# A decoder layer: a zero column ahead of the attention's keys, packed bytes moved as 32-bit words, and the 384-column tile's values issued earlier on TensorE

## The reference, cut to what matters

```python
q = (x @ Wq).reshape(B, T, H, Dh)
k = (x @ Wk).reshape(B, T, H, Dh)
v = (x @ Wv).reshape(B, T, H, Dh)
scores = jnp.einsum('bthd,bshd->bhts', q, k)
mask = jnp.tril(jnp.ones((T, T), dtype=scores.dtype))
scores = scores * mask
attn = jax.nn.softmax(scores / T ** 0.5, axis=-1)
out = jnp.einsum('bhts,bshd->bthd', attn, v).reshape(B, T, H * Dh)
...
low = W_packed & 15
high = W_packed >> 4 & 15
```

## Time and profile before

| | |
|---|---|
| median of three runs | 1464.04 us |
| the profiled execution: its own time | 1464.93 us |
| the profiled execution: its span | 1463.2 us |
| TensorE busy | 1418.3 us, 97% |
| VectorE, ScalarE, GpSimd busy | 992.6, 711.9, 386.7 us |
| exponentials (L1269) | 256, and 256 reads of their sums |
| `exp_zero` (L1278) | 48 |
| pack casts on ScalarE and VectorE | 16 each |
| conversions of bytes on GpSimd (L759) | 96 |

### The profile page before, as it was taken

How to read it: one execution, slowest core, us unless ns; L and a number is a source line. 1 busy time by engine, 2 the same in 40 slices (tenths; PEclk the granted TensorE clock), 3 DMA queues, 4 the chain that set the end, 5 groups by cost and what they waited for, 6 DMA issues and landing times.

```text
span 1463.2 us, 26832 instructions
## 1 busy us (share of the span) xinstructions
PE 1418.3 (97%) x8896; PEld 718.8 (49%) x8896; DVE 992.6 (68%) x2125; ACT 711.9 (49%) x1648; POOL 386.7 (26%) x703
## 2 busy tenths in 40 slices
PE   6999999999999999999999999999999999999999
PEld 4466457456645644344444444444444444444444
DVE  7796788679568868885675566666666665766533
ACT  5795289249527944345344353353353343443432
POOL 0054225305473545421121121211112112212100
PEclk9999999999999999999999999999999999999999
DMA  7554612452556601010100100001001001000011
GB/s 252 136 173 122 177 67 89 126 145 67 157 147 182 206 32 45 17 33 17 33 17 17 33 17 17 23 12 35 17 17 33 17 17 33 17 17 1 1 58 58
DMA packets 77310, 98.01 MB, mean 67 GB/s; under 512 B 8049, under 2 KB 60785, under 8 KB 76785
## 3 DMA queue, kind: packets, MB, share of 16 engines
q1 hardware_dynamic: 77168, 96.23, 21.5%
HBM read 68.94 MB, written 27.26 MB: 66 GB/s over the span
## 4 chain that ended last, share of the span: by engine, by line
PE 87%; DVE 5%; ACT 4%; issue 3%; DMA 0%; POOL 0%; DVEq 0%; ACTq 0%; POOLq 0%; SPq 0%
PE bank L888 25%; PE bank L890 25%; PE bank L889 25%; PE bank L952 3%; PE bank L973 2%; ACT prob L1269 2%; PE bank L941 2%; PE bank L982 1%; PE bank L901 1%; PE bank L1013 1%; PE bank L1028 1%; PE bank L1023 1%; DVE xt L1595 1%; ACT pk_t L1303 1%; DVE bank L1610 1%
## 5 line engine op out<-in xcount | busy, mean ns | idle before, releaser
L888 PE MATMUL bank<-xs,G 128*128 128x512 f16 x896 | 339.8, 379 | 2.1 <-DVE c L1741 0.9
L889 PE MATMUL bank<-xs,G 128*128 128x512 f16 x896 | 339.6, 379 | 0.0
L890 PE MATMUL bank<-xs,G 128*128 128x512 f16 x896 | 339.6, 379 | 0.0
L1741 DVE TENSOR_TENSOR c<-bank,c 128x512 f32<-128x512 f32 x128 | 88.1, 689 | 193.0 <-PE bank L890 193.0
L1355 ACT COPY c<-bank 128x512 f32<-128x512 f32 x192 | 111.4, 580 | 220.4 <-PE bank L890 215.5
L888 PE MATMUL bank<-Wd,hid 128*128 128x512 f16 x512 | 194.1, 379 | 2.8 <-DVE X L1795 2.8
L889 PE MATMUL bank<-Wd,hid 128*128 128x512 f16 x512 | 194.0, 379 | 0.0
L890 PE MATMUL bank<-Wd,hid 128*128 128x512 f16 x512 | 194.0, 379 | 0.0
L751 POOL TENSOR_TENSOR c<-c,m 128x512 f32<-128x512 f32 x64 | 82.4, 1288 | 388.5 <-ACT c L1355 388.5
L1795 DVE SCALAR_TENSOR_TENSOR X<-bank,col,X 128x512 f32<-128x512 f32 x128 | 95.3, 749 | 101.6 <-PE bank L890 101.5
L1610 DVE CUSTOM_DVE_ANT_0 bank<-bank,mask,col 128x128 f32<-128x128 f32 (+3 forms) x256 | 139.2, 548 | 21.3 <-PE bank L941 12.1
(11 more groups left out here) (196 smaller groups left out, 2397.4 us busy)
## 6 DMA issues: line engine op xcount, KB each, us to landing
stack<-qk_dram SPq DMA_DIRECT2D x128, 128.0 KB, 3.3
sc_in<-scale_t SPq DMA_DIRECT2D x30, 384.0 KB
qk_dram<-qk SPq DMA_DIRECT2D x32, 256.0 KB, 3.1
packed_t<-pk_t SPq DMA_DIRECT2D x32, 192.0 KB, 2.0
pk_in<-packed_t SPq DMA_DIRECT2D x30, 192.0 KB
X<-in_x_dram SPq DMA_DIRECT2D x4, 1024.0 KB, 6.1
pk_in<-L_ffn_gate_W_packed_dram SPq DMA_DIRECT2D x16, 256.0 KB, 2.8
pk_in<-n_L_ffn_up_W_packed_dram SPq DMA_DIRECT2D x16, 256.0 KB, 3.1
```

The costliest lines, as they stand in the source:

```text
L888: pe.matmul(o, lhs(0), rhs(0), start=first, stop=False, skip_group_check=onto)
L889: pe.matmul(o, lhs(0), rhs(1), start=False, stop=False, skip_group_check=onto)
L890: return pe.matmul(o, lhs(1), rhs(0), start=False, stop=stop, skip_group_check=onto)
L1741: nc.vector.tensor_tensor(dst[:], bank[at][:], dst[:], ALU.add).then_inc(comb, 1)
```

## The change

1. The keys get two zero columns ahead of each head's 512. For the three narrower tiles the score matmul begins one column early, so column 0 of the bank is the score 0 and the keys follow in columns 1 to `wide`. `row_max` works on columns 1 and up, the exponential on all `wide + 1`, so that `prob[..., 0]` is exp(-max) and the sum holds it once. `exp_zero`, `e_zero` and its semaphore go. `all_tokens` and `masked_values` read `prob[..., 0]`, the turns read their blocks one column further on, and each exponential from the third unit on waits for `den_done` and `v_zero_done` of two units before. GpSimd clears the zero columns once.
2. `convert` adds 1024 to each byte in place of the plain cast, so the fp16 value holds the byte in its low eight bits. `repacked` on ScalarE copies 384 fp32 words instead of casting 768 columns, `repacked` on VectorE copies 768 fp16 columns without a cast.
3. `recips` and `values` of the 384-column tile (units 2, 6 and 10, `sooner`) are issued after the turn of the third head of the 512-column tile, ahead of its fourth head and of the next unit's fourth scores. The slots are counted accordingly.

```diff
-        stack = sb("stack", [P, 2, HEADS, T], F16)
+        stack = sb("stack", [P, 2 * HEADS * T + 2 * HEADS], F16)
+        queries = stack[:, 0:HEADS * T].rearrange("p (h t) -> p h t", h=HEADS)
+        keys = stack[:, HEADS * T:].rearrange("p (h t) -> p h t", h=HEADS)
...
         def turn_slot(h):
-            return h + 2 * (max(0, h - 2) // 16) + max(0, h // 4 - 1)
+            return h + 2 * (max(0, h - 2) // 16) + max(0, h // 4 - 1) + int(h % 16 == 15 and h < ROWS - 1)
...
+        def sooner(u):
+            return u % TT == TT - 2 and u < UNITS - 2
+
         def recip_slot(u):
-            return turn_slot(4 * u + 7) + 1 if u < UNITS - 1 else pack_slot(HG - 1, 1) + 1
+            if u == UNITS - 1:
+                return pack_slot(HG - 1, 1) + 1
+            return turn_slot(4 * u + (6 if sooner(u) else 7)) + 1
...
-                        sp.dma_start(stack[32 * part:32 * part + 32, which, 4 * c:4 * c + 4, :],
+                        sp.dma_start((queries, keys)[which][32 * part:32 * part + 32, 4 * c:4 * c + 4, 2 * which:2 * which + T],
...
+            pool.wait_ge(w_lo, W_PARTS)
+            nc.gpsimd.memset(keys[:, :, 0:2], 0.0).then_inc(zero_keys, 1)
...
-                nc.gpsimd.tensor_copy(pk_16[:, a], pk_in[:, a].bitcast(U8).rearrange("p (c four) -> p c four", four=4)[:, :, 0]).then_inc(pk_conv, 1)
+                nc.gpsimd.tensor_scalar(pk_16[:, a], pk_in[:, a].bitcast(U8).rearrange("p (c four) -> p c four", four=4)[:, :, 0],
+                                        BYTES, None, ALU.add).then_inc(pk_conv, 1)
...
-                    pool.wait_ge(e_zero_done, beyond_units(n, u - 2))
...
-                pool.wait_ge(e_zero_done, beyond_units(n, u))
+                pool.wait_ge(exp_done, n * ROWS + 4 * u + 4)
...
-                                        e_zero[:, u % 2, :].unsqueeze(2).to_broadcast([P, 4, DH]), ALU.mult).then_inc(v_zero_done, 1)
+                                        prob[:, u % 2, :, 0:1].to_broadcast([P, 4, DH]), ALU.mult).then_inc(v_zero_done, 1)
...
-                pe.matmul(bank[j][:, 0:wide[i]], stack[:, 0, h, P * i:P * i + P], stack[:, 1, h, 0:wide[i]],
+                pe.matmul(bank[j][:, 0:wide[i] + beyond[i]], queries[:, h, P * i:P * i + P], keys[:, h, 2 - beyond[i]:2 + wide[i]],
...
-                    mm = pe.transpose(turn_bank(slot)[:, P * k:P * k + P], prob[:, u % 2, j, P * k:P * k + P], ident[:])
+                    at = P * k + beyond[i]
+                    mm = pe.transpose(turn_bank(slot)[:, P * k:P * k + P], prob[:, u % 2, j, at:at + P], ident[:])
...
-                        if j == 3 and u > 0:
+                        if j == 2 and u > 0 and sooner(u - 1):
+                            recips(n, u - 1)
+                            values(n, u - 1)
+                        if j == 3 and u > 0 and not sooner(u - 1):
                             recips(n, u - 1)
                             if u < UNITS - 1:
                                 values(n, u - 1)
...
                 if u >= 2:
                     act.wait_ge(t_full, n * ROWS + 4 * (u - 2) + j + 1)
-                nc.scalar.activation(prob[:, u % 2, j, 0:wide[i]], bank[j][:, 0:wide[i]], ACT.Exp,
-                                     bias=nmx[:, u % 2, j:j + 1], accum_out=den[:, u % 2, j:j + 1]).then_inc(exp_done, 1)
-
-            def exp_zero(n, u):
-
-                if u >= 2:
                     act.wait_ge(den_done, beyond_units(n, u - 2))
                     act.wait_ge(v_zero_done, beyond_units(n, u - 2))
-                act.wait_ge(shift_done, n * ROWS + 4 * u + 4)
-                nc.scalar.activation(e_zero[:, u % 2, :], nmx[:, u % 2, :], ACT.Exp).then_inc(e_zero_done, 1)
+                nc.scalar.activation(prob[:, u % 2, j, 0:wide[i] + beyond[i]], bank[j][:, 0:wide[i] + beyond[i]], ACT.Exp,
+                                     bias=nmx[:, u % 2, j:j + 1], accum_out=den[:, u % 2, j:j + 1]).then_inc(exp_done, 1)
...
-                nc.scalar.copy(pk_t[:, 0], turn_bank(pack_slot(r, 0))[:].bitcast(F16)[:, 0:HALF]).then_inc(pk_out0, 1)
+                nc.scalar.copy(pk_t[:, 0].bitcast(F32), turn_bank(pack_slot(r, 0))[:, 0:HALF // 2]).then_inc(pk_out0, 1)
...
-                        if j == 3 and u % TT < TT - 1:
-                            exp_zero(n, u)
...
-                nc.vector.tensor_copy(pk_t[:, 1], turn_bank(pack_slot(r, 1))[:].bitcast(F16)[:, 0:HALF]).then_inc(pk_out1, 1)
+                nc.vector.tensor_copy(pk_t[:, 1].bitcast(F16), turn_bank(pack_slot(r, 1))[:].bitcast(F16)[:, 0:HALF]).then_inc(pk_out1, 1)
```

More of the change, by code:

```diff
@@ L137, in decoder_layer @@
         v_beyond = sb("v_beyond", [P, TT - 1, D], F32)
-        w_raw = stack[:].rearrange("p a h t -> p (a h t)").bitcast(F32).rearrange("p (w k n) -> p w k n", w=4, k=KT)
+        w_raw = stack[:, 0:2 * HEADS * T].bitcast(F32).rearrange("p (w k n) -> p w k n", w=4, k=KT)
         xn = sb("xn", [P, TT, D], F32)
@@ L152, in decoder_layer @@
         r_den = sb("r_den", [P, 2, P], F32)
-        e_zero = sb("e_zero", [P, 2, 4], F32)
         v_zero = sb("v_zero", [P, 2, P], F32)
@@ L223, in decoder_layer @@
         c11 = [sb2(f"c11_{x}", [P, T], F32) for x in range(2)]
+        sb2("beside_zero_keys", [P, HEADS], F32)
         G[1] = sb2("G1", [P, 7, 2, 4, P], F16)
@@ L250, in decoder_layer @@
         qkv_full, qk_hi, qk_lo, v_out = (sem(n) for n in ("qkv_full", "qk_hi", "qk_lo", "v_out"))
-        vb_full, vb_out, e_zero_done, v_zero_done = (sem(n) for n in ("vb_full", "vb_out", "e_zero_done", "v_zero_done"))
+        vb_full, vb_out, zero_keys, v_zero_done = (sem(n) for n in ("vb_full", "vb_out", "zero_keys", "v_zero_done"))
         stacked = [sem(f"stacked{i}") for i in range(4)]
@@ L277, in decoder_layer @@
         wide = [(i + 1) * P for i in range(TT)]
+        beyond = [int(i < TT - 1) for i in range(TT)]
         def turn_slot(h):
-            return h + 2 * (max(0, h - 2) // 16) + max(0, h // 4 - 1)
+            return h + 2 * (max(0, h - 2) // 16) + max(0, h // 4 - 1) + int(h % 16 == 15 and h < ROWS - 1)
         def copied_by_act(u):
@@ L317, in decoder_layer @@
         AHEAD = 4
+        BYTES = 1024.0
         CONTEXT_BANK = (6, 4, 5, 7)
@@ L930, in scores @@
                 hg, i = u // TT, u % TT
+                if n + u + j == 0:
+                    pe.wait_ge(zero_keys, 1)
                 if i == 0 and j == 0:
@@ L1608, in row_max @@
                 alone(dve, s_full, n * ROWS + 4 * u + j + 1)
-                nc.vector.tensor_tensor_reduce(out=bank[j][:, 0:wide[i]], in0=bank[j][:, 0:wide[i]],
+                own = slice(beyond[i], beyond[i] + wide[i])
+                nc.vector.tensor_tensor_reduce(out=bank[j][:, own], in0=bank[j][:, own],
                                                in1=mask[:, P * (3 - i):P * (3 - i) + wide[i]], scale=C_EXP,
@@ L1626, in all_tokens @@
                     dve.wait_ge(exp_done, n * ROWS + 4 * u + 4)
-                    dve.wait_ge(e_zero_done, beyond_units(n, u))
-                    nc.vector.scalar_tensor_tensor(den_all[:, u % 2, :], e_zero[:, u % 2, :], float(T - wide[i]), den[:, u % 2, :],
+                    nc.vector.scalar_tensor_tensor(den_all[:, u % 2, :], prob[:, u % 2, :, 0], float(T - wide[i] - 1), den[:, u % 2, :],
                                                    ALU.mult, ALU.add).then_inc(den_done, 1)
```

## The result

The kernel after takes 1477.74 us (median of four runs, 1476.16 to 1477.85), the kernel before beside it 1464.32. The ratio is 1.0086, with the interval 1.0073 to 1.0099: slower, by 13.4 us. The forecast was 1460.2 with a range of 1458.8 to 1464.4; the measured time lies above it, on the other side of the kernel before.

The account below looks back on a forecast made before the run. ScalarE was taken to bound the attention loops' 384- and 512-column stages, cross-engine waits the narrow ones. Savings of 1.5 (zero column), 2.3 (packed bytes) and 0 (moved values) made 3.8 us: 1460.2, range 1458.8 to 1464.4.

Parts of the forecast that it names:

- Half rate on odd columns: TensorE's score matmuls on fp16 keys from an odd column: taken as free, at worst half rate, 1.9 us.
- Rival (c): Attention loop: the fourth head's scores, 0.73 us later, hold up the repack; slower, 1469 if wholly paid; chance 0.1.
- I count its saving in full: Attention loops: TensorE's work behind each waits only for the loop, so all its saving, 3.8 us in sum, counts.
- I take 0.40, as it has one input like the cast: GpSimd's byte conversion as a one-input TENSOR_SCALAR: still 0.40 us, so no loss.
- It matters in one place: GpSimd's conversion delays only the third head's shift and exponential: 1.2 us per 0.1 us more per conversion.
- The upper bound of 0.74: GpSimd's conversion at worst like a two-input TENSOR_TENSOR of 256 columns: 0.34 us more each, 4.1 us in all.
- Rival (a): Slower GpSimd conversion or half-rate odd columns eat the gain: typically 1462.5, at worst 1466; chance 0.3 shared with another rival.
- L759 [...] over 0.5 means (a): Sign in GpSimd's conversion row: 0.40 us confirms the forecast, over 0.5 means costs eat the gain.

Follow-up runs that it names:

- experiment 2: Kernel after with the plain cast on GpSimd and both pack casts as before, leaving zero column and moved values: 1461.94 us, ratio 0.9982.
- experiment 5: Kernel after with only GpSimd's conversion put back to the plain cast (wrong codes, same instructions and sizes): 1460.33 us, ratio 0.9968.
- experiment 3: Kernel before with only the values of the 384-column tile moved: 1464.53 us, ratio 0.9998.
- experiment 6: The integer version: kernel after, but GpSimd casts bytes to int16, ScalarE copies int32 words and VectorE int16 columns; 1460.17 us, ratio 0.9966.
- experiment 7: Kernel before with each GpSimd conversion split into a TENSOR_SCALAR of 128 columns and a cast of 128: 1475.69 us, one execution.
- experiment 12: Kernel after with its conversions evened out over the 384- and 512-column units, none ahead of its load: 1472.15 us, ratio 1.0046.
- experiment 1: Kernel before with only GpSimd's byte conversion replaced by the TENSOR_SCALAR that adds 1024: 1480.71 us, ratio 1.0110.
- experiment 9: Kernel after with its conversions moved to units where GpSimd idles, two of six into the 256-column unit: 1490.87 us, ratio 1.0174.

## Why the prediction was wrong

**What held.** Part 1 was put at -1.5 us and gave 2.15 in the median (0.47 a loop, 1.9, by the stages), in the stages named. Half rate on odd columns did not happen. Part 2's copy on ScalarE was put at -2.3: 0.19 a group, 12 times, is what the stages show, and the medians of experiments 2 and 5 differ by 1.6. Part 3 was put at 0 +-0.05 a group and gave 0.06 to 0.07. Rival (c) did not come: the repack starts 2.04 us behind the stage's first exponential in experiment 3, and 2.09 in experiment 6, where it was 2.11 (the 1.75 of the kernel after lies in a stage that the slow conversion has shortened). With the conversion at its old price the time is that of the forecast, 1460.33 and 1460.17 (experiments 5 and 6) for 1460.2. That it fits so closely is in part luck: parts 1 and 3 gave more than forecast, part 2 by the medians less, and the four loops of experiment 6 are shorter by 4 x 1.27 = 5.1 us, not 3.8, of which the median shows 4.4 against the kernel before beside it. "I count its saving in full" is thus not borne out exactly; no run says where the rest goes.

**What failed** is one step: GpSimd's conversion, "I take 0.40, as it has one input like the cast", and "It matters in one place [...] Each 0.1 us more per conversion would cost 12 x 0.1 = 1.2 us". It is wrong in three ways.

- The price. The upper bound of 0.74 came from two-input instructions, and I took it for safe because this one has a single input. The row is 857 ns, above the bound. The number of inputs was no measure: here the cast is the fast one, and the operation with arithmetic as slow as one with two inputs. The Trainium skill, GPSIMD Engine Reference, section Elementwise, side-by-side cycle accounting, gives about 1.8 cycles per element for a tight loop and 2.6 for two inputs; at the 1.2 GHz that the page gives, an estimate from these is 1.5 and 2.2 ns. Experiment 7 shows 2.7 ns a column, and 2.5 by the durations alone, above both, so the page pointed the right way and not far enough.
- What surrounds it. A duration is not a distance between starts. I wrote so for ScalarE and did not apply it to GpSimd: 0.46 us more of duration became 0.73 more from shift to shift.
- The places. I priced the one shift that is tight now, and its slack only. Six conversions stand in the two wide stages. GpSimd's list there took 6.12 us in the integer version (101.57 to 107.69) with waits of 0.45, 0.68 and 0.21 us in it, so 4.78 of work. Six times 0.73 make 4.4 more: 9.2, against the 7.56 us of the stages (3.43 + 4.13). The engine passes from 63% to over 100% of these stages, and then no place is slack; measured 9.11, and 8.86 in the last sequence. I could have read this from the earlier trace rows (2.56 + 2.65 us busy of 7.67) with the price alone. At my own upper bound of 0.34 more each it would have said 7.25 of 7.67, near enough to full to widen the range.

**The sum with the right step.** A group with both wide stages grows by 1.28 and 0.27 us; the first group, which has no `out_head`, by less, and the last group's 512-column stage by nothing. In the last sequence, where the fourth shift of that unit takes 0.19 us and not 0.48 (experiment 12), the 512-column stage stays at 4.14 and the 128-column stage at 2.93. In the other three the 128-column stage after them is 0.33 shorter (2.99 to 2.66), which I put down to TensorE and VectorE running ahead while ScalarE waits (no run takes that apart). In all the first loop is 60.42 against 55.94 (the others are 4.46 to 4.61 longer), so 4 x 4.48 = 17.9 us, against 17.6 between the medians of the kernel after and of experiment 6. Less the 4.2 us that the other parts gain (1464.32 to 1460.17), that is the 13.4 of the result.

Rival (a) had the right cause, a slower conversion where GpSimd has no slack, and at most 4.1 us for it; the cost was four times that. The sign to look for was named ("L759 [...] over 0.5 means (a)") and came.

## What to carry to other kernels

When an operation on a helper engine becomes dearer, sum that engine's whole list over the stretch in which its work stands, waits taken out, and compare it with the stretch; a slack in one place says nothing once the sum is full, and a 30% average over the span hides it. The sum is a lower bound: in experiment 7 a short stretch paid though the whole was not full. Price a changed operation by the distance between starts, and treat a bound from another operation as no bound. Before work is moved to an idle gap, look when its input lands and what stands behind it in the same list. If only bits are to be moved, a cast between integer types did it at the old price where an addition doubled it.

## What the runs showed of the hardware

- GpSimd's TENSOR_SCALAR with one input: 857 ns on average at 128x256 (0.85 us in 91 of 96 rows) and 558 at 128x128 (0.53 us in 81 of 96), 2.7 ns a column from start to start, against 0.7 for its CAST (396 to 398 ns at 256). Reading bytes four apart or 32-bit words makes no difference. It starts some 0.15 us later behind a shift than a cast does.
- Score matmuls whose fp16 keys start at an odd column: 334, 274 and 229 ns at 385, 257 and 129 columns, against 331, 274 and 227 at 384, 256 and 128 before.
- A GpSimd shift that started while VectorE ran its TENSOR_SCALAR over 128x512 fp32 (0.54 us) lasted longer: not 0.19 us, but 0.48 in the kernel after, 0.37 in the kernel before and 0.24 in experiment 12, nine times in each, and ended 0.04 to 0.05 us behind VectorE's instruction. In experiment 1 it was eight times of nine; the ninth shift began within 0.05 us of VectorE's start and took 0.19. The two go together in the rows; no run moved VectorE's instruction to test it.
- TensorE's granted clock fell to 0.50 (1.2 GHz) in five of the twelve groups of experiment 9, after idles of 1.73 to 2.27 us in an otherwise busy loop, and not after one of 2.04. Each of the five 384-column stages took 1.1 to 1.2 us more than the seven at full clock. The edit had moved work on GpSimd alone.
- ScalarE's copy of 384 int32 words from a bank takes 482 ns, of 384 fp32 words 483. VectorE's copy of 768 16-bit columns takes 555 ns as fp16, 556 as int16 and 556 with the cast of before.
